# Deformable convolution with three taps sampled densely and six gathered, for two and seven, and one addition of GpSimd before a gather for two

## What is computed

```python
o = softmax(q @ k.T * scale) @ v             # per image and head, 4096 x 4096
x = proj(o) + x
om = conv3x3(W_off @ concat(x, 2 * feat_s)) + b_om
py, px = y - 1 + ky + off_y, x - 1 + kx + off_x      # per pixel, group (8) and tap (9)
y0, x0 = floor(py), floor(px); ly, lx = py - y0, px - x0
val = gather(y0, x0) * (1-ly) * (1-lx) + gather(y0, x0+1) * (1-ly) * lx \
    + gather(y0+1, x0) * ly * (1-lx) + gather(y0+1, x0+1) * ly * lx     # 0 outside the image
val = val * sigmoid(mask)
out = relu(einsum('bgckhw,ogck->bohw', val, W_dcn) + b_dcn) + x
```

## Time and profile before

| | us |
|---|---|
| three runs | 12688.98, 12680.93, 12687.91 (median 12687.91) |
| profiled execution, its own time | 12682.99 |
| its span, first to last instruction | 12681.2 |
| TensorE busy (matmuls) | 9257.2 |
| DVE busy | 7291.4 |
| ACT busy | 4747.5 |
| GpSimd busy | 10320.1 |
| gathers (L469), 7168 of them | 7156.6 |
| additions of GpSimd (L465), 13824 of them | 3063.5 |
| mean granted TensorE clock | 0.838 of full speed |

### The profile page before, as it was taken

The page is one execution under the profiler, slowest core; times in us unless marked ns, Lnnn a source line. Parts: engine busy times, 40 slices in busy tenths (PEclk is TensorE's granted clock), DMA queues, the critical chain, the costliest instruction groups (busy, mean ns, idle before and its releaser), DMA issues. The chain is left out here.

```text
span 12681.2 us, 168047 instructions
## 1 busy us (share of the span) xinstructions
PE 9257.2 (73%) x56052; PEld 5057.7 (40%) x56052; DVE 7291.4 (57%) x10291; ACT 4747.5 (37%) x6104; POOL 10320.1 (81%) x21509
## 2 busy tenths in 40 slices
PE   4677778775778777776577777777577777777754
PEld 1244444442444444443244344444234444444444
DVE  4356566644666666664566666665456666666443
ACT  1344444432434434433244344343233434334322
POOL 0278888885788888888488888888858888888888
PEclk7888888886888888888788888888788888888876
DMA  1222211110011111111011111111101111111100
GB/s 48 77 67 70 66 23 24 24 24 23 21 33 25 24 24 25 25 24 29 13 25 33 24 24 25 25 23 24 28 16 31 25 25 25 25 23 24 24 22 21
DMA packets 373774, 373.51 MB, mean 29 GB/s; under 512 B 129440, under 2 KB 219936, under 8 KB 372768
## 3 DMA queue, kind: packets, MB, share of 16 engines
q0 software_dynamic: 229376, 235.34, 8.9%
q10 hardware_dynamic: 97920, 71.35, 1.8%
q1 hardware_dynamic: 45472, 54.53, 1.6%
HBM read 316.66 MB, written 44.04 MB: 28 GB/s over the span
## 5 line engine op out<-in xcount | busy, mean ns | idle before, releaser
L469 POOL DMA_INDIRECT g<-patches,idx x7168 | 7156.6, 998 | 1112.4 <-issue 949.5
L905 DVE TENSOR_REDUCE mx<-ring 128x2 f32<-128x1024 f32 x2048 | 2411.1, 1220 | 2919.3 <-PE ring L666 2381.8
L541 ACT ACTIVATE p<-ring 128x1024 f32<-128x1024 f32 x2048 | 1984.8, 1021 | 3832.3 <-PE ring L724 2960.3
L465 POOL TENSOR_TENSOR carrier<-carrier 128x1 f32<-128x1 f32 x13824 | 3063.5, 250 | 122.0
L708 PE MATMUL ps_x<-fx,hats 128*128 128x208 f32 x12288 | 2520.1, 356 | 120.4 <-DVE hats L1048 78.8
L721 PE MATMUL ring<-qf,kf 32*128 32x512 f32 x8192 | 1459.9, 786 | 1515.3 <-ACT hats L551 816.3
L708 PEld LDWEIGHTS ps_x<-fx,hats 128*128 128x128 f32 x12288 | 2192.2, 196 | 671.2 <-issue 598.1
L734 PE MATMUL ps_a<-p,v 128*64 128x512 f32 x4096 | 1442.3, 790 | 39.0 <-DVE shared L932 37.6
L734 PE MATMUL ps_b<-p,v 128*64 128x512 f32 x4096 | 1247.2, 692 | 0.0
L1067 DVE TENSOR_TENSOR ps_x<-ps_x,chosen 128x416 f32<-128x416 f32 x1024 | 611.1, 597 | 1053.2 <-PE ps_x L708 844.1
L574 ACT COPY vt<-ps_x 128x256 f32<-128x256 f32 (+1 forms) x512 | 204.5, 399 | 2659.1 <-PE ps_x L780 1505.9
(11 more groups left out here) (125 smaller groups left out, 7601.4 us busy)
## 6 DMA issues: line engine op xcount, KB each, us to landing
g<-patches,idx POOLq DMA_INDIRECT x7168
patch_in<-in_fpad ACTq DMA_DIRECT2D x544, 64.0 KB
patches<-patch_out ACTq DMA_DIRECT2D x136, 256.0 KB
fx<-in_fpad SPq DMA_DIRECT2D x20, 416.0 KB
p<-in_x SPq DMA_DIRECT2D x4, 2048.0 KB
xq<-in_x SPq DMA_DIRECT2D x32, 256.0 KB
fs_s<-in_fs SPq DMA_DIRECT2D x32, 256.0 KB
xs<-in_x SPq DMA_DIRECT2D x32, 256.0 KB
```

The costliest lines, as they stand in the source:

```text
L465: last = nc.gpsimd.tensor_tensor(carrier[:, col:col + 1], carrier[:, 0:1], carrier[:, 0:1], ALU.add)
L469: nc.gpsimd.indirect_dma_start(out=g[:, j, :], out_offset=None, in_=patches[b], in_offset=bass.IndirectOffsetOnAxis(ap=idx[:, t, j:j + 1], ...
L541: nc.scalar.activation(p[:, (2 * kt + pair) % 4, :, :], ring[slot][:, :, :], ACT.Exp, scale=SCALE)\
L905: V.tensor_reduce(mx[:, n:n + 2, c], ring[slot][:, :, :], AX.X, ALU.max).then_inc(ring_free[slot], 1)
```

## The change

`DENSE` goes from 2 to 3. So a tile has 48 gathers instead of 56 (parts of 2, 2, 1 and 1 taps), 6 sets instead of 4, and 12 halves instead of 8. `SET_AT` becomes 0, 1, 2, 4, 5, 6: in key tiles 1, 2, 5 and 6 of a window the second half of one set and the first half of the next stand together, and the order in `halves_at` is turned so that the older set's half comes first. `hats` gets a third buffer, and ACT does the two Relus (`cut_hats`) right behind the Abs of the same set instead of one key tile later. Before a gather stands one addition of GpSimd (`RESTS` = 1). The transposed taps are laid in `vt` in the order in which the parts bring them (`SLOT_TAPS`): the first dense tap goes with the third part, the two others with the fourth.

```diff
-DENSE = 2
+DENSE = 3
 PICKED = TAPS - DENSE
 PARTS = 4
 CUTS = tuple(min(2 * part, PICKED - (PARTS - part)) for part in range(PARTS + 1))
-LAST_TAPS = CUTS[PARTS] - CUTS[PARTS - 1] + DENSE
+DENSE_CUTS = (0, 0, 0, 1, DENSE)
+WIDTHS = tuple(CUTS[part + 1] - CUTS[part] + DENSE_CUTS[part + 1] - DENSE_CUTS[part] for part in range(PARTS))
+SLOTS = tuple(sum(WIDTHS[:part]) for part in range(PARTS))
+SLOT_TAPS = tuple(tap for part in range(PARTS) for tap in (*range(CUTS[part], CUTS[part + 1]),
+                                                           *range(PICKED + DENSE_CUTS[part], PICKED + DENSE_CUTS[part + 1])))
+HATS = 3
...
-RUN, RESTS = 1, 2
+RUN, RESTS = 1, 1
...
-        hats = sb("hats", [128, 2, 1 + PAIRS, SET_GROUPS * 128])
+        hats = sb("hats", [128, HATS, 1 + PAIRS, SET_GROUPS * 128])
...
         def halves_at(s, kt):
-            return tuple((r, t, i, half) for half in range(2) for r, t, i in sets_with(s, kt, half))
+            return tuple((r, t, i, half) for half in (1, 0) for r, t, i in sets_with(s, kt, half))
...
-                    for r, t, i in weighed_at(s, kt):
-                        cut_hats(uses, t, i)
...
                     for r, t, i in hats_at(s, kt):
                         distances_to_hats(uses, t, i)
+                        cut_hats(uses, t, i)
...
-                for tap in range(TAPS):
-                    last = mm(aligned, wdcn_s[:, tap, :], vt[:, tap, :], start=tap == 0, stop=tap == TAPS - 1)
+                for k, tap in enumerate(SLOT_TAPS):
+                    last = mm(aligned, wdcn_s[:, tap, :], vt[:, k, :], start=k == 0, stop=k == TAPS - 1)
...
-                if part == PARTS - 1:
-                    for d in range(DENSE):
-                        last = tr(turned[:, (picked + d) * 128:(picked + d + 1) * 128], dval[:, t % 2, d * C:(d + 1) * C],
-                                  ident_s[:, :])
+                for k, d in enumerate(range(DENSE_CUTS[part], DENSE_CUTS[part + 1]), picked):
+                    last = tr(turned[:, k * 128:(k + 1) * 128], dval[:, t % 2, d * C:(d + 1) * C], ident_s[:, :])
```

More of the change, by code:

```diff
@@ L325, in build @@
         assert all(slots_in(o) % 2 == 0 for o in (FIRST, MID, LAST))
-        assert MID[-1][0] == "rows" and MID[0][0] == ("scores", 0)
+        assert ("rows", 2) in MID and MID[0] == (("scores", 0), 2)
         BATCH_SLOTS = USES_KV + slots_in(FIRST) + (STEPS_B - 2) * slots_in(MID) + slots_in(LAST)
@@ L547, in distances_to_hats @@
                 (slot,) = uses.slots(name)
-                made = hats[:, i % 2, :, :]
+                made = hats[:, i % HATS, :, :]
                 nc.scalar.activation(made[:, 0, :], ring[slot][:, 0, :], ACT.Abs, bias=plus_x, scale=-1.0)
@@ L571, in keep_turned @@
                 m = part_number(r, t, part)
-                width = 128 * (LAST_TAPS if part == PARTS - 1 else CUTS[part + 1] - CUTS[part])
+                width = WIDTHS[part] * 128
                 act.wait_ge(val_turned, m + 1)
-                nc.scalar.copy(vt[:, CUTS[part]:CUTS[part] + width // 128, :].rearrange("p k n -> p (k n)"), turned[:, 0:width]).then_inc(vt_ready, 1)
+                nc.scalar.copy(vt[:, SLOTS[part]:SLOTS[part] + WIDTHS[part], :].rearrange("p k n -> p (k n)"), turned[:, 0:width]).then_inc(vt_ready, 1)
             def step(s, b, i):
@@ L707, in blocks_of_half @@
                     for pair in range(PAIRS):
-                        last = mm(cells, hats[:, i % 2, 1 + pair, j * 128:(j + 1) * 128], fx[:, pair, :, group * GC:(group + 1) * GC],
+                        last = mm(cells, hats[:, i % HATS, 1 + pair, j * 128:(j + 1) * 128], fx[:, pair, :, group * GC:(group + 1) * GC],
                                   start=pair == 0, stop=pair == PAIRS - 1)
```

## The result

The changed kernel took **14708.9 us** (median of four runs, 14703.61 to 14716.05) against 12684.42 for the kernel before on the same chip: a ratio of **1.160**, 95% interval 1.158 to 1.162. It is 16% slower. The forecast was 15,180, the range 13,950 to 15,900.

The account below looks back on a forecast made before the run. GpSimd's gathers were taken as the bound (360 us a step), another chain 3% behind at 350. Adding 99 us to that chain gave about 450 a step, +2489 us over the run: about 15,180 us, range 13,950 to 15,900.

Parts of the forecast that it names:

- a second chain: TensorE, ACT and DVE waiting on each other over PSUM's two ring slots: about 350 us a step without gathers in the way.
- GpSimd's side: Gathers and additions on GpSimd: spacing falls from 1.47 to 1.33 us, its bound from 360 to about 280 us a step.
- 1, second halves: Key tiles 1, 2, 5, 6: second half waits for DVE to read the first in `half_set`; 14.2 us a tile.
- M: The start of the maxima matmuls in a key tile, from which the prediction counted its times.
- 2 and 3, distances, clock and Relus: Two more distances (key tiles 3, 7), 6.3 us a tile; low-clock scores behind distances and Relus before exponentials, 4.5 us a tile.
- The rival in which the clock stays up: Denser key tiles keep TensorE at 2.4 GHz: 413 us a step, about 14,050 us in all; chance 0.10.
- 4 and 5: `weigh_hats` before `points`, 2.6 us a step; one tap less to sample, taken at 0; last key tile, -4 us a step.
- 21 ordinary steps: Steps between RECIPROCALs going from 360.2 to about 450 us each, 1886 us over the run.
- three early steps: Two steps where ACT also copies patches, +100 us each, and the one before them with three tiles of four, 75.
- last step of four images: Each image's last step, without maxima to compute: 402 us for 359, 43 each, 172 in all.
- behind the last step: The run's end, attention over and gathers setting the pace: 540 us of gathers become 418, -120 us.
- the rival with the busy shares: New work fits into TensorE's 79 idle us a step: 327 us a step, about 11,750 us in all; chance 0.07.

Follow-up runs that it names:

- the fillers: The changed kernel with two additions before a gather, plus ten zero-weight products of 512 columns on TensorE behind each set of distances: 14797.31 us.
- the late Relus: The changed kernel with two additions before a gather, ACT doing a set's two Relus one key tile later, behind the next exponentials: 14760.96 us.

## Why the prediction was right, and where it was off

**The bound now.** Right: the gathers were the bound, and a second chain stood closely behind. DVE's wait for gathered data (10.4 us a step) gave 350 us for that chain; 343 was measured. Such a wait counts only what is late at one place. The 7 us by which it was missed are not accounted for; that late data stretch a step at other places too, without a wait in their name, is a guess.

**GpSimd's side.** The step that it falls to 280 us and bounds nothing holds: it is busy 242 us of 430 and the two additions put back cost 3 us. Its foreseen busy time of 7,700 us is 7,735. But the sentence that there is no reason for the spacing to stay above 1.47 us was wrong for the kernel before, where one addition alone costs 24%. It did no harm here, and that was luck and not insight. Why the changed kernel stays clear of the late signals is open. One would look for it in GpSimd's waits for `val`, which cut the gathers short. Counted in stretches in which each gather starts under 1.4 us after the one before, the changed kernel has one over 30 us (60 us, in the beginning), and its 37 others over 20 us end after 16 to 18 gathers. The kernel before with one addition has 241 over 20 us and 24 over 30, up to 49 us, and the two kernels without second halves or distances, in which the late signals came back, have 21 and 28 over 30 us. But the length of a stretch can't be all of it. In the changed kernel TensorE changed a semaphore 706 times more than 10 us into such a stretch, and none of these was late; in the kernel before with one addition it was 849 times, and 678 were more than 3 us late.

**1, second halves.** The forecast was M + 4.65 for the start of the second one and M + 6.95 for TensorE going on; the trace has M + 4.53 and M + 6.73. (The prediction's own terms, 0.95 + 2.35 + 1.2, make M + 4.50; and from M + 3.1 to M + 6.95 it is 3.85 us, where it counted 3.7.) 14.2 us a tile were forecast, and 15.6 measured by taking them away. This term carries the result.

**2 and 3, distances, clock and Relus.** This is the term that was too large: 6.3 + 4.5 = 10.8 us a tile, 43 a step, of which taking two distances away gave back 20. The distances themselves are as forecast: key tile 3 ends at M + 6.52 (5607.10), where it was M + 3.53 in the earlier trace rows, 3.0 for a forecast 3.2. What failed is the price of the clock. It was taken from one key tile, 6.06 us from the scores to the maxima at the lower clock against 3.48, so 2.6, and counted for six such places in a tile, less a quarter. In the changed kernel the slow key tile takes 4.79 (5595.79 to 5600.58) and the fast one behind distances 4.05 (5607.10 to 5611.15, with its wait of 0.82), for 3.39 without either. So a place behind distances costs 1.4 or 0.7 us here, not 2.6. The trace of before has the same: from scores behind distances to the maxima its median is 4.80 us, 1.3 more than the 3.48 of scores without a gap, and 35 of the 239 reach 6 us. The next such place in the earlier trace rows, the scores at 4661.55, was at the maxima 4.60 us later. One of the slowest was taken for all. The share at half pace, from the granted clock, fell from 0.26 x 360 = 94 us (0.87) to 0.16 x 430 = 69 us (0.92), where half as many distances again were expected to bring more of it.

The rival in which the clock stays up was thus half true. It would have given 413 us a step; the fillers show why even a clock of 0.96 gives 434: ACT's Relus come last in its place. The Trainium skill, "TensorE: Matmul & The Clock Gate", has activity release the clock (What's actually happening) as well as pauses throttle it (HAM oscillation). The prediction weighed the second. This case's traces agree with the first in that a step with TensorE busy 317 us for 281 had a granted clock of 0.92 for 0.87; with the second in part, as behind gaps of 2 to 3.2 us scores at half pace and at full pace both occur, 104 and 282 of 399.

**4 and 5.** The sum of the measured pieces is 343 + 62.4 + 20 = 425 us, and the step is 430.1 with one addition and 433.3 with two. The 5 to 8 us between them have to hold `weigh_hats` ahead of `points` (2.6 us in the prediction, without a working), the tap less to sample, and the clock of the old places. They were not told apart, and the pieces need not add up exactly. So of the step's parts, base, second halves, distances with clock and Relus, and the rest, the forecast had 350, 57, 43 and -1 us, and 343, 62, 20 and 5 to 8 were measured: the first, second and last errors are small, and the third makes most of the 20 us.

**Over the run.** The spans differ by 2026 us, forecast 2489:

| | forecast | measured |
|---|---|---|
| 21 ordinary steps | 1886 | 1504 (71.6 each) |
| three early steps | 275 | 315 |
| three with an image's start | 276 | 234 |
| last step of four images | 172 | 81 |
| behind the last step | -120 | -110 |

The first row has the sizes above. The two early steps where ACT copies patches were 25 us each worse than forecast: ACT's Relus ahead of the exponentials cost there, as the late Relus showed. The last step of an image was forecast from a chain of 303 us, 359 less the 55.6 of DVE's waits; with fewer gathers that step took 313, and as DVE still waited 16 to 18 us for gathered data in it, its chain alone was not measured. So at least 67 us were added to it, and hardly 99: taking the wait off here too gives some 83, an estimate. The granted clock there rose from 0.82 to 0.90, and without maxima nothing takes the place of what a faster clock saves: the fillers, too, gained 16 us there and nothing elsewhere.

Faster, the rival with the busy shares, would have needed second halves to fall in TensorE's idle time. TensorE has 113 us of it in a step now, 79 before: the new work did not fill gaps, it brought its own.

## What to carry to other kernels

When an engine is the bound, measure how far behind the next chain stands before work is moved off it: here 17 us of 360, and the work that was moved brought 87 to the chain. A piece of work put on a chain costs its waits and not its busy time; two users of one buffer in a row cost the round over the reader (3.78 us from one half to the next, for 2.38 of matmuls). And operations that look useless, such as additions of one column between gathers, can hold a rate down on which other engines depend: take them away alone, once, before the change is built on it.

## What the runs showed of the hardware

- Beside indirect DMAs that GpSimd issues 1.33 us apart for tens of microseconds, the semaphore changes of TensorE, and of ACT and DVE none, arrive up to tens of microseconds late (12.7, 25 and 31.5 us in the stretch shown), with the DMA engines 11% busy. TensorE itself goes on until it waits for an engine that waits for it. In the kernel before at 1.47 us, or with 1.34 us of additions once in 11.8 us, none is late; with 0.76 us in their place (mean 1.40) they are. It cost 24% and 14%. The changed kernel has stretches of 20 us at the same 1.33 us and none late. What the two share on the way is open.
- Behind gaps of 2 to 3.2 us scores ran at half pace in 103 of 239 places and, in the changed kernel, in 104 of 399. Fillers, which left gaps of 0.36 and 1.65 us in the two places looked at, brought a step from 0.91 to 0.96 of the clock and did not shorten it.
- In two kernels an idle time that was taken off TensorE (5 and 15 us a step) went with 8.5 and 11 us a step more of busy time for the same matmuls, at a granted clock of 0.89 and 0.88 for 0.91.
